# A transformer layer on one core: SyncE's list of a slot in another order, and its large copies in pieces

## What is computed

```python
x = layernorm(x + attn(x, x, x, causal=True))          # 16 heads of width 8
x = layernorm(x + attn(x, ctx, ctx, causal=False))
x = layernorm(x + moe(x))                              # top 2 of 8 experts, each 128 -> 512 -> 128, GELU
```

## Time and profile before

| what | us |
| --- | --- |
| median of 3 runs | 750.6 |
| runs | 745.12 to 751.87 |
| the profiled execution, its own time | 756.12 |
| its span | 754.3 |
| TensorE busy / VectorE busy / ScalarE busy / GpSimd busy | 574.4 / 491.6 / 437.6 / 358.9 |

### The profile page before, as it was taken

The page is one execution under the profiler, slowest core; times in us unless marked ns, Lnnn a source line. Parts: engine busy times, 40 slices in busy tenths (PEclk is TensorE's granted clock), DMA queues, the critical chain, the costliest instruction groups (busy, mean ns, idle before and its releaser), DMA issues. The chain is left out here.

```text
span 754.3 us, 21229 instructions
## 1 busy us (share of the span) xinstructions
PE 574.4 (76%) x7870; PEld 455.7 (60%) x7870; DVE 491.6 (65%) x1345; ACT 437.6 (58%) x814; POOL 358.9 (48%) x564
## 2 busy tenths in 40 slices
PE   2578777866867778997798888867698788777990
PEld 1255555554544557676576676655598677677880
DVE  4288898974998767777887679996632424221253
ACT  1254564543534448998699789867666664444320
POOL 7133334332444843444477356728852573540360
PEclk9998897886996869999799999997999999999995
DMA  4454347474322455554556646634357888988730
GB/s 99 131 186 133 95 122 218 143 258 123 103 61 79 124 178 160 158 165 126 152 169 170 197 128 201 181 93 141 115 172 243 267 283 262 292 257 265 228 101 28
DMA packets 142310, 124.65 MB, mean 165 GB/s; under 512 B 12225, under 2 KB 124625, under 8 KB 142209
## 3 DMA queue, kind: packets, MB, share of 16 engines
q1 hardware_dynamic: 134496, 113.06, 49.9%
q0 software_dynamic: 4176, 8.53, 4.1%
q10 hardware_dynamic: 3536, 1.70, 0.8%
HBM read 86.81 MB, written 38.54 MB: 166 GB/s over the span
## 5 line engine op out<-in xcount | busy, mean ns | idle before, releaser
L1212 DVE TENSOR_REDUCE row_max<-bank 128x16 bf16<-128x1024 f32 x64 | 78.2, 1222 | 44.0 <-PE bank L1627 42.9
L1767 PE MATMUL bank<-w_in,w_hl 128*128 128x128 f32 x704 | 98.9, 284 | 0.0
L1004 ACT ACTIVATE probT<-bank 128x1024 f32<-128x1024 f32 x64 | 65.6, 1024 | 51.9 <-PE bank L1652 50.9
L887 POOL TENSOR_TENSOR prob_lo<-probT,prob_hi 128x384 f16<-128x384 f32 x64 | 66.4, 1038 | 48.7 <-ACT prob_hi L1007 48.4
L1767 PEld LDWEIGHTS bank<-w_in,w_hl 128*128 128x128 f32 x704 | 86.6, 194 | 0.2
L873 POOL TENSOR_TENSOR veps<-mv,eps 128x1 f32<-128x1 f32 x64 | 15.1, 236 | 145.6 <-DVE mv L1250 145.6
L1056 ACT ACTIVATE w_hl<-bank 128x512 f32<-128x512 f32 x88 | 52.6, 598 | 43.9 <-PE bank L1753 43.4
L1753 PE MATMUL bank<-xT,w_in 128*128 128x128 f16 x1056 | 74.5, 221 | 0.0
L896 POOL DMA_INDIRECT xs<-x_hl,pos x60 | 63.6, 1060 | 21.9 <-issue 17.2
L912 POOL DMA_INDIRECT w_hl<-ys,pos x52 | 51.8, 996 | 46.0 <-DMA ys<-w_hl 31.6
L1677 PE MATMUL bank<-consts,o_n 128*128 128x64 f32 x256 | 45.2, 303 | 30.4 <-DVE o_n L1231 26.8
(11 more groups left out here) (182 smaller groups left out, 1547.5 us busy)
## 6 DMA issues: line engine op xcount, KB each, us to landing
w_in<-w_scr SPq DMA_DIRECT2D x96, 512.0 KB, 4.4
q_scr<-q_hl SPq DMA_DIRECT2D x64, 128.0 KB, 2.1
k_scr<-k_hl SPq DMA_DIRECT2D x64, 128.0 KB, 2.7
q_st<-q_scr SPq DMA_DIRECT2D x32, 256.0 KB, 3.1
k_all<-k_scr SPq DMA_DIRECT2D x128, 64.0 KB, 2.5
xs_tile<-xs SPq DMA_DIRECT2D x42, 128.0 KB, 5.0
ys<-w_hl SPq DMA_DIRECT2D x42, 128.0 KB
xs<-xs_tile SPq DMA_DIRECT2D x3, 1472.0 KB, 7.3
```

The costliest lines, as they stand in the source:

```text
L887: pool.tensor_tensor(p_lo[u.buf][:, h, :], probT[u.buf][:, h, :], p_hi[u.buf][:, h, :], ALU.subtract).then_inc(lo_second[u.kind], 1)
L1004: act.activation(probT[u.buf][:, :, :].rearrange("p h q -> p (h q)"), bank[:, KEYS:KEYS + 2, :].rearrange("p a n -> p (a n)"), ACT.Exp, sc ...
L1212: dve.reduce_max(row_max[u.buf][:, :], bank[:, SC:SC + 2, :].rearrange("p a (h k) -> p (a h) k", k=S), AX.X).then_inc(max_done[a], 1)
L1767: last = pe.matmul(expert_y(x), hid[x.par][:, c, :], w2_t[x.wb][:, c, :], start=False, stop=c == FC - 1, skip_group_check=True)
```

## The change

In `slot` the token loads, the clearing and the expert copies move from the head of SyncE's list to behind the fetches and the first loads of an opening chunk (ahead of the late weights and the expert weights). Each chunk's clearing becomes pieces of four tiles (256 KB; the last piece of a chunk has three), 23 in all, one in each slot from 4 to 26. The expert copies become 16 pieces of 256 KB, one in each slot from 11 to 26: in slots 11, 13, ... the first weights of expert 0, 1, ... (from SBUF), in slots 12, 14, ... the second weights of the same expert (DRAM to DRAM). A first-weights piece waits only for its own expert's split. The scatters and the first row loads wait for all 23 clearings, the first tile's weights for all 16 copies.

```diff
-CLEAR_SLOT, CLEAR_EVERY = 10, 2
+CLEAR_SLOT, KEEP_SLOT = 4, 11
...
-def cleared_at(slot):
-    return next((c for c in range(DENSE) if CLEAR_SLOT + CLEAR_EVERY * c == slot), None)
+CLEARED = [(c, k, min(4, TILES_OF[c] - k)) for c in range(DENSE) for k in range(0, TILES_OF[c], 4)]
...
-        FIRST_WEIGHTS, WEIGHTS, LATE_WEIGHTS, MOE_WEIGHTS, KEPT = 6, 6, 13, 5, 2
+        FIRST_WEIGHTS, WEIGHTS, LATE_WEIGHTS, MOE_WEIGHTS, KEPT = 6, 6, 13, 5, 2 * E
...
-            def keep_experts():
-
-                v = w_scr.rearrange("(e p) f -> p e f", e=E)
-                sp.wait_ge(w1_lo_ready, E)
-                sp.dma_start(v[:, :, 0:FF], w1_hl[:, :, :, :].rearrange("p e s f -> p e (s f)").bitcast(f32)).then_inc(moe_kept, 16)
-                sp.dma_start(w_scr[:, FF:FF + FC * D], w["e_w2"]).then_inc(moe_kept, 16)
-
-            def clear_rows(c):
-
-                sp.dma_start(xs[c].rearrange("(k p) f -> p k f", p=P), xs_t[0][:, 0, :].unsqueeze(1).to_broadcast(
-                    [P, TILES_OF[c], 2 * D])).then_inc(cleared, 16)
+            def keep_expert(e, second):
+
+                r = slice(e * P, (e + 1) * P)
+                if second:
+                    sp.dma_start(w_scr[r, FF:FF + FC * D], w["e_w2"][r, :]).then_inc(moe_kept, 16)
+                else:
+                    sp.wait_ge(w1_lo_ready, e + 1)
+                    sp.dma_start(w_scr[r, 0:FF], w1_hl[:, e, :, :].rearrange("p s f -> p (s f)").bitcast(f32)).then_inc(moe_kept, 16)
+
+            def clear_rows(c, k, n):
+
+                sp.dma_start(xs[c][k * P:(k + n) * P, :].rearrange("(k p) f -> p k f", p=P), xs_t[0][:, 0, :].unsqueeze(1).to_broadcast(
+                    [P, n, 2 * D])).then_inc(cleared, 16)
...
             def slot(g):
-                for b in range(2, NBLK):
-                    if prepared_at(b, 0) - (3 if b < 5 else 2) == g:
-                        load_tokens(SELF, Block(b))
-                if b := cross_tokens_at(g):
-                    load_tokens(CROSS, b)
-                if g == W1_SLOT + E + 2:
-                    keep_experts()
-                if (c := cleared_at(g)) is not None:
-                    sp.wait_ge(zeroed, ZEROED)
-                    clear_rows(c)
-
                 self_b = prepared(g - 1, 1)
                 cross_q, cross_k = crossed(g - 1, 1), crossed(g - 1, 2)
...
                 for x in by_rows:
                     load_pair_rows(x)
+                for b in range(2, NBLK):
+                    if prepared_at(b, 0) - (3 if b < 5 else 2) == g:
+                        load_tokens(SELF, Block(b))
+                if b := cross_tokens_at(g):
+                    load_tokens(CROSS, b)
+                if 0 <= (k := g - CLEAR_SLOT) < len(CLEARED):
+                    sp.wait_ge(zeroed, ZEROED)
+                    clear_rows(*CLEARED[k])
+                if 0 <= (k := g - KEEP_SLOT) < 2 * E:
+                    keep_expert(*divmod(k, 2))
                 if g == 1:
                     load_late_weights()
```

More of the change, by code:

```diff
@@ L738, in load_pair_rows @@
                 sp.wait_ge(scattered[x.c], 16 * 2 * NT[x.c])
-                sp.wait_ge(cleared, 16 * DENSE)
+                sp.wait_ge(cleared, 16 * len(CLEARED))
                 if x.pair >= XB:
@@ L892, in scatter @@
                 n = PAIRS * FIRST_BLK[c] + t
-                pool.wait_ge(cleared, 16 * DENSE)
+                pool.wait_ge(cleared, 16 * len(CLEARED))
                 pool.wait_ge(pos_ready, c + 1)
```

## The result

Over four runs each, shown in the table, the changed kernel takes 738.99 us against 751.24, ratio 0.9854 with a 95% interval of 0.9818 to 0.9890: about 11 us less, between 8 and 14.

What follows compares the result with a forecast made beforehand. The prediction took two TensorE stalls before scores (slots 18 and 20), waiting for k behind large copies, as what the change could save. Gain 10 us, all else at no cost: 750.6 - 10 = 740.6 us, range 736 to 747.

Steps and rivals of the forecast that it cites:

- three estimates: Saving in slots 14 to 21: by idle times 10.4 us, by four-slot stretches 9.5, by VectorE's share 12.5 or 9.9.
- estimate (b): Slots 14 to 17 and 18 to 21 against copy-free slots 22 to 25: 3.4 and 6.1 us too much, sum 9.5.
- estimate (a): TensorE's two idle times before scores, slots 18 and 20, alone: 4.28 + 6.10 = 10.4 us.
- What is late next: Slots 14 to 21: once the stalls go, VectorE, the busiest engine there, is late next; 10 us gain taken.
- Order at no cost: Slots 4b+4: k send moves 2.8 us ahead of the token load; later token loads cost nothing.
- Pieces at no cost: SyncE's queue: 33 more issues, 0.7 us a slot, and 512 KB costing 2.1 us, hidden by slack: cost nothing.
- The last pieces: Slot 26 pieces, which the first scatter in slot 27 awaits: cost 0 to 0.7 us, taken as 0.
- The signs: No idle before scores in slots 18, 20; k sent before tokens, fetched 3 to 4 us later; slots 14 to 21 some 54.
- One sign of being wrong: Slots 14 to 26: among the signs against the forecast, sends whose two issues take over 2 us.
- Half of it: Slots 14 to 17's excess may be clock and casts; only slots 18 to 21 give 6.1 us: 744.5; chance 0.25.
- The clock adds to it: Slots 14 to 21: returning clock adds 5.3 us, gain 15.7, time 734.9; chance 0.13.
- slower rival: Self blocks 6 to 9: each small piece pays its own landing, delaying q and k; 14 us slower, 764.6; chance 0.07.

Runs made afterwards that it cites:

- c: Kernel before with only the expert copies as pieces at the end of SyncE's list, token loads and whole clearings still at the head: ratio 0.9882 to before.
- d: Kernel before with only the clearing as pieces at the end of SyncE's list, token loads and whole expert copies still at the head: ratio 0.9935 to before.
- second profile of before: Unchanged kernel before, run and profiled once more: ratio 0.9987 to before; slots 14 to 25 took 92.4 us.
- e: Changed kernel with the token loads back at the head of SyncE's list, pieces at its end: ratio 0.9875 to before.
- a: Kernel before with only the order changed: token loads, whole clearings and whole expert copies behind the fetches: ratio 0.9856 to before.
- f: Changed kernel with the pieces at the head of SyncE's list, ahead of the sends, and token loads at its end: ratio 0.9864 to before.
- g: Changed kernel with each 256 KB piece cut into four transfers of 64 KB, issued together: ratio 1.0032 to before.
- b: Kernel before with clearing and copies in pieces, but token loads and pieces still at the head of SyncE's list: ratio 0.9833 to before.
- j: Changed kernel with each expert copy piece written three times into a wider scratch, as many transfers: ratio 0.9920 to before.
- i: Changed kernel with each 256 KB piece cut into two transfers of 128 KB: ratio 0.9875 to before.

## Why the prediction was right

*What bounded the kernel.* The two waits of `scores` were the transfers of k, held up by the clearing and the expert copies. Shown: taking away either copy from ahead of the send takes away its stall and no other (c, d).

*The size.* I forecast 10 us from three estimates of 10.4, 9.5 and 9.9 to 12.5. In slots 14 to 21 the trace of before and that of after differ by 64.6 - 55.1 = 9.5, which is estimate (b); against the second profile of before it is 66.3 - 55.1 = 11.2, which is the sum of that profile's two idle times, the way of estimate (a). The timed gain, 8 to 14 us, does not choose between them. The further 7.3 us of the profiled executions are chance, and the forecast was right not to count on such.

*What is late next.* VectorE, as forecast: it is busy 25.05 of 27.1 us in slots 18 to 21, and TensorE waits 5.4 us more for `max_diag` than in the first profile of before. That sum alone tells little: the second profile has 26.1 us of it, only 2.5 less than the changed kernel.

*Order at no cost.* The k send came 4.6 us ahead of the token load (2.8 forecast), the low half being ready at 139.85. The 4.6 us are not what the turn-in would have cost: the token load now stands behind the fetch, which ended at 144.50. In e, with the token load first, k goes out at 142.62, 3.5 us after its low half (138.64 + 0.45), and that costs nothing that shows, as forecast. In a, where order makes the gain, the whole copies move behind the sends too, so a does not price the token loads alone.

*Pieces at no cost.* Right at 256 KB, in front of the sends or behind them (f), but the slack that I gave as the reason was the wrong one to watch. I set the pieces against the time that k has in hand and put SyncE's 0.7 us a slot of issuing aside; g shows that issuing is what runs out first. The price of bytes, 2.1 us for 512 KB, came out near: in b, behind 512 KB, k of cross block 2 took 4.6 us from send to fetch, 1.8 more than in the changed kernel, and j's added 512 KB a slot cost 2.4 and 3.7.

The rule of the Trainium skill, "DMA: Bandwidth & Descriptors", section "Rules for kernel authors", to join small transfers and to make them 1 MiB and more did not decide here: pieces of 256 and 128 KB were free, with others waiting in the same queue. The fixed 2 us a transfer that the Trainium skill gives (same page, section "Latency and other measured facts") are mostly the time until the landing is confirmed, by that section. This agrees with the 64 KB pieces of g, which land in 1.7 to 2.3 us and yet go out every half microsecond: it is no time for which the queue is held.

*The last pieces.* SyncE issued the last copy at 219.01 and GpSimd began its first scatter at 224.62, 5.6 us later, with the same 0.36 us of idle time as before. Cost 0.

*The signs.* In slots 10 to 26 k was fetched 2.8 to 3.8 us after its send, near the 3 to 4 given; slots 14 to 21 took 55.1 us, a little more than the 54 given. One sign of being wrong did show, at no cost: k of slot 26 took 2.25 us for its two issues (at 212.37), and no `scores` waited for it.

*The rivals.* "Half of it" falls with d: the first stall alone was worth 0.65% (0.34 to 0.97). "The clock adds to it" falls too: the granted clock of slots 18 to 21 did return from 0.72 to 0.94 and TensorE's busy time from 24.51 to 20.72, but the stretch is no shorter than the 27 us of its neighbours; slots 14 to 17 ran at 0.82, lower than before (0.86), and still took 3.6 us less. In i, slots 14 to 17 and 18 to 21 take the same time at two mean granted clocks, 0.87 and 0.94:

```profile
126.20:153.20 27.00, 22.11 (x335) 15.25 (x329) 25.07 (x56) 14.86 (x29) 10.69 (x20) 0.87 0.50 143
153.20:180.30 27.10, 20.75 (x338) 14.84 (x332) 25.06 (x59) 14.16 (x28) 11.94 (x23) 0.94 0.59 168
```

That activity releases the clock, as "TensorE: Matmul & The Clock Gate" (Part 1) of the Trainium skill has it, agrees with these rows. In the changed kernel it gave back nothing that the rows show; the likely reason is VectorE, busy 25 of the 27 us in both. Slots 14 to 17 of c, above, may be an exception. The slower rival's mechanism, a landing paid by each small piece, is not what happens at 64, 128 or 256 KB; its outcome does come at quarter pieces, by another way.

## What to carry to other kernels

On a queue that runs in order, look at what was issued just ahead of each transfer that somebody waits for, and price a large copy there by the time from send to fetch with and without it; a wait whose releaser the profile cannot name may be such a transfer. Here moving the copy behind the urgent transfers and cutting it did the same job, so try the cheaper edit first. Cut only until the issuing engine's own spare time is used up: count its issues over a slot and the time that it still waits for work to be ready.

## What the runs showed of the hardware that I had not expected

Here the issuing engine, not the transfers, sets how small the pieces may be: 64 KB transfers issued 0.45 to 0.6 us apart each landed in about 2 us and did not hold up one another, yet 62 more of them in twelve slots cost 15.5 us. Two issues behind the 4 MB of copies took 4.5 to 4.9 us in place of 0.9 (before in both profiles, a, d), and two right behind a whole clearing, in slots 12 and 16, 4.7 to 5.5 in place of 1.2 (before in both profiles, c): an issue itself can be held up by what stands in its queue, and with it everything behind it on the engine.
